# One row for the value groups and the state's update: a reordering of a fused attention and network kernel

## The chip, the cores and the metric

The kernel runs on one core of a Trainium2 chip. The metric is the device time of one launch in microseconds (us). The kernel before took 996.28 us, the median of three runs (994.85 to 998.28).

## The reference, cut to what matters

x has 4 sequences of 1024 tokens with 512 features. It is normalised (xn), and two branches are added to it.

```python
xn = layernorm(x)
q, k = rotary(xn @ Wq), rotary(xn @ Wk);  v = xn @ Wv       # 16 heads of 32
# attention with decay, by chunks of 128 tokens, for each head:
inter  = (q * q_decay) @ kv                    # kv: the state, 32 x 32
scores = (q @ k.T) * dmask                     # 128 x 128
attn   = inter + scores @ v
kv     = r_C * kv + (k * k_decay).T @ v
x1 = rms_norm(attn, rms_w) @ Wo
# a network with sparse hidden values:
z = xn @ ternary(W_syn).T + b_syn              # 2048 wide
hidden = where(z >= 204th largest of the row, relu(z), 0)
x2 = layernorm(xn + hidden @ ternary(W_out).T + b_out, gamma, beta)
out = x + x1 + x2
```

## The kernel before, in words

The 4096 tokens are 32 tiles of 128, and a tile is one chunk of the attention. After a prologue that loads and converts the weights, `run_steps` writes out 31 steps, and `last_steps` does what is left. Each engine has its own queue, whose order is written out by hand in its `step`. Semaphores are the only ties between them: `wait(eng, name, tile, per, n)` waits until the semaphore stands at tile.n x per + n. A step works on five tiles at once: a (two ahead: it is loaded and normalised), b (one ahead: q, k, v and z), t (attention, and the search for the threshold), u (one behind: threshold, hidden values, output projection) and d (two behind: the network's second product and the result).

**TensorE** (`step`, L1014): second product of the network for d, high half, the failure flag of u, low half; transposes of q; three chunks of q, k, v for b (12 products each); the state's part of the attention (`earlier_values`); scores of three groups of four heads; the output projection of u (`attention_projected`, 12 products); the first chunk of z (`projection(b, 3)`, 8 products); the scores of the fourth group; values of groups 0 and 1; second z chunk; values of groups 2 and 3; third z chunk; the update of the state (L1051); fourth z chunk; the sum of squares. The projections, z, the scores and the network use 128 columns of the array. `values` (L951) and the update (L1051) use 32 columns at a time, four heads side by side, in float32.

The scores go to three banks, `SCORES = [1, 2, 0, 1]`, so that the fourth group's bank is free when VectorE has scaled the first group (`P_ready`). The chunks of q, k, v and z share two banks, `proj`: a z chunk waits until the chunk two places ahead of it has been copied out (`qkv_out` by ScalarE for chunks 3 and 4, `z_out` by VectorE for chunks 5 and 6).

**VectorE** (`step`, L1488): last z chunk of t, flag, state, mean square, threshold of u (with a branch, for rows whose search failed), `hidden` (L1413), decayed q, statistics of a, first step of the search, result of the network for d, normalised attention, second step; then `below` (L1461), which writes all values of z under a bound to `masked`; `probs` 0 and 1, which scale the scores into `Pr`; four MAX8 (`segments`); `out_shift` of d (L1455); z chunk 0; `probs` 2 and 3; MAX8; z chunk 1; the projected attention added to x; MAX8; z chunk 2; MAX8; and `selection` (L1464 to L1486), a chain of small instructions on the 128 candidates that picks the threshold with `sel` (L1479).

`Pr` has two buffers of four heads, which the groups use in turn, so group 2 waits for the values of group 0. The same memory is `unused`, to which ScalarE's three counts write results that nobody reads; so `probs` waits for the third count (`sum3`).

**ScalarE** (`step`, L548): `diagonal`, `first_count`, `hidden_high` (L533), first copy of q (`qkv_out(b, 0)`, L427), the heads of the state (`heads_state`, L457, four instructions), `second_count` (L519), `attention_high` (L410), `normalised` (L436 and L439: x normalised in float32, and its float16 half), `third_count` (L524), `qkv_out` 1 and 2 (L427), `out_normalised` (L538, needs `out_shift`), `attention_out` (L544 and L546: the attention `aT` and its squares `sq`, both from the values' bank), `qk_high` (L447).

**GpSimd** (`step`, L736): root of the mean square (L702), decayed v (L745), decayed state (L751), root for the statistics (L634), `hidden_low` (L708), `attention_low` (L712), `low_half` (L640, needs both results of `normalised`), `out_root` of d (L716, gives `rD_ready`), biases (L645, L646), rotary (L658 to L663), `squares_added` (L721, L723), `out_scaled` and `out_added` (L728, L734), `qk_low` (L668, twice).

**SP** issues the transfers: high and low halves of the hidden values transposed, x transposed (needs `low_half`), result stored, next x loaded, q and k transposed (need `qk_low`).

Of the kernel before, what the change touches and what calls it, by code (L numbers as in the profile page):

```python
# [26 lines left out]
H, DH = 16, 32  # L27
# [5 lines left out]
NT = 32  # L33
# [17 lines left out]
def build(nc, x, Wq, Wk, Wv, Wo, rms_w, W_syn, b_syn, W_out, b_out, gamma, beta,  # L51
          t_rot, t_dmask, t_qdec, t_kdec, t_rc, t_keep, t_ident, t_iota, out):
    ctx = ExitStack()
    with ctx:
        def sb(name, shape, dt):
            return ctx.enter_context(nc.sbuf_tensor(name, shape, dt))[:]
# [54 lines left out]
        pair_a = sb("pair_a", [P, 2 * E], F32)  # L111
        aT = pair_a[:, 0:E].rearrange("p (g c) -> p g c", g=HG)
        sq = pair_a[:, E:2 * E].rearrange("p (g c) -> p g c", g=HG)
        state = sb("state", [P, P], F32)
        stateD = sb("stateD", [P, HG, P], F32)
        kvs = sb("kvs", [P, P], F32)
# [50 lines left out]
        SCORES = [1, 2, 0, 1]  # L167
# [193 lines left out]
        def _(act):  # L361
# [154 lines left out]
            def second_count(t):  # L516

                wait(act, "nt_step", t, 5, 2)
                nc.scalar.activation(unused, z[:, t.par, :], ACT.Sign, bias=nt1, accum_out=s2).then_inc(S["sum2"], 1)  # L519
# [28 lines left out]
            def step(act, i, p):  # L548
                a, b, t, u, d = (stage(i, p, k) for k in (2, 1, 0, -1, -2))
                tile0 = t.n == 0  # L550
                if u:
                    diagonal(u)
                first_count(t)
                if t.n == 1:
                    heads_state(t)
                if u:
                    hidden_high(u, masked)
                if b.n >= 3:
                    qkv_out(b, 0)
                if t.n > 1:  # L560
                    heads_state(t)
                second_count(t)
                if u:
                    attention_high(u)
                if a:
                    normalised(a)
                third_count(t)
                if tile0:
                    sums("out", (1, 2, 3, 0))
                    sign("out", out_in[2], out_other[2], out_thr[1])  # L570
                    sign("out", out_in[2], out_t[2], out_thr[0])
                else:
                    if b.n != 2:
                        qkv_out(b, 1)
                    qkv_out(b, 2)
                if d:
                    out_normalised(d)
                attention_out(t)
                if tile0:
                    act.wait_ge(S["out_tern3"], 1)  # L580
                    sign("out", out_in[1], out_other[1], out_thr[1])
                    sign("out", out_in[1], out_t[1], out_thr[0])
                qk_high(b)
                if tile0:
                    qkv_out(Tile(1, 0), 0)
                    qkv_out(Tile(1, 0), 1)

                    act.wait_ge(S["out_tern2"], 1)
                    sign("out", out_in[0], out_other[0], out_thr[1])
                    act.wait_ge(S["outT3"], 16)  # L590
                    sign("out", out_in[0], out_t[0], out_thr[0])
# [32 lines left out]
        def _(pool):  # L624
# [84 lines left out]

            def attention_low(u):  # L710
                wait(pool, "ah_ready", u, 1, 1)
                nc.gpsimd.tensor_tensor(ahl[:, 1], aT, ahl[:, 0], ALU.subtract).then_inc(S["al_ready"], 1)  # L712

            def out_root(d):
# [78 lines left out]
        def _(pe):  # L793
# [152 lines left out]
            def values(t, g):  # L946

                wait(pe, "P_ready", t, 4, g + 1)
                for j in range(4):
                    h = 4 * g + j  # L950
                    last = nc.tensor.matmul(p_av[32 * j:32 * j + 32, g * P:(g + 1) * P],  # L951
                                            v[:, t.par, h * DH:(h + 1) * DH], Pr[:, g % 2, j, :],
                                            start=False, stop=g == HG - 1, skip_group_check=True)
                last.then_inc(S["av_done"], 1)

# [58 lines left out]
            def step(pe, i, p):  # L1014
                b, t, u, d = (stage(i, p, k) for k in (1, 0, -1, -2))
                if d:
                    network_high(d)
                if u:
                    failures(u)
                if d:  # L1020
                    network_low(d)
                if t.n > 0:
                    q_transposed(t)
                if b.n > 1:
                    for n in range(2 if b.n == 2 else 0, 3):
                        projection(b, n)
                        if n == (2 if b.n == 2 else 0):
                            factors_spread(u)

                earlier_values(t)  # L1030
                scores(t, 0)
                scores(t, 1)
                scores(t, 2)
                if u:
                    attention_projected(u)
                projection(b, 3)
                scores(t, 3)
                values(t, 0)
                values(t, 1)
                projection(b, 4)  # L1040
                values(t, 2)
                values(t, 3)
                if t.n == 0:
                    sums_spread("out")
                projection(b, 5)

                wait(pe, "vd_ready", t, 1, 1)
                wait(pe, "P_ready", t, 4, 2)
                for h in range(H):
                    g, j = h // 4, h % 4  # L1050
                    last = nc.tensor.matmul(sbank[2][32 * j:32 * j + 32, g * DH:(g + 1) * DH],  # L1051
                                            qk[:, t.par, E + h * DH:E + (h + 1) * DH],
                                            vd[:, h * DH:(h + 1) * DH], start=True, stop=True)
                last.then_inc(S["kv_done"], 1)
                projection(b, 6)
                if t.n == 0:
                    projection(Tile(1, 0), 0)
                    projection(Tile(1, 0), 1)
                squares_summed(t)
# [71 lines left out]
        def _(dve):  # L1131
# [188 lines left out]
            def probs(t, g):  # L1320

                wait(dve, "scores_done", t, 4, g + 1)

                wait(dve, "av_done", t, 4, g - 1)
                wait(dve, "sum3", t, 1, 1)
                nc.vector.scalar_tensor_tensor(Pr[:, g % 2].rearrange("p j c -> p (j c)"), sbank[SCORES[g]], ppp,  # L1326
                                               dmask[:, 4 * g:4 * g + 4, :].rearrange("p j c -> p (j c)"),
                                               ALU.mult, ALU.mult).then_inc(S["P_ready"], 1)

# [158 lines left out]
            def step(dve, i, p):  # L1488
# [37 lines left out]
                below(t)  # L1526
                if tile0:
                    dve.wait_ge(S["dmask_loaded"], 16)
                probs(t, 0)
                probs(t, 1)  # L1530
                segments(t, 0)
                if d:
                    out_shift(d)
                z_chunk(b, 0)
                probs(t, 2)
                probs(t, 3)
                segments(t, 1)
                z_chunk(b, 1)
                if u:
                    attention_added(u)  # L1540
# [147 lines left out]
```

## Time and profile before

| what | value |
|---|---|
| median of three runs | 996.28 us (994.85 to 998.28) |
| the profiled execution: time, span, granted clock | 997.11 us, 994.4 us, 0.985 |
| TensorE matmul busy (instructions) | 941.7 us, 95% (6771) |
| VectorE busy | 847.6 us, 85% (2294) |
| GpSimd busy | 759.2 us, 76% (653) |
| ScalarE busy | 584.0 us, 59% (777) |
| chain that ended last, TensorE's share | 86% |

The profile is of one execution. The span is the time between the first and the last instruction on the core. Busy shares are averages over prologue, steps and tail. L12 is line 12 of the kernel; PE is TensorE, DVE VectorE, ACT ScalarE, POOL GpSimd. Consecutive matmuls overlap, so the distance from the start of one group to the start of the next is what a group costs, and not its length.

### The profile page before, as it was taken

The page shows a single profiled execution, that of the slowest core. Times are in us where ns is not written, and L with a number is a line of the kernel's source. Part 1 is how long each engine was busy: PE and PEld are TensorE (multiplying, and loading weights), DVE is VectorE, ACT ScalarE, POOL GpSimd, SP SyncE. Part 2 cuts the span into 40 slices and gives each one's busy share as a digit, 9 for nine tenths or more (in the row PEclk, how much of TensorE's full clock was granted, in tenths as well). Part 3 has the DMA queues.
Part 4 walks back from the last instruction along what each step waited for, and adds up shares of the span by engine and source line. Part 5 has one row for each costly group of instructions (what it writes and reads, how often), then busy time and mean ns, then how long its engine had stood idle before and what let it go on. Part 6 is the DMA issues. An engine that isn't in the chain of part 4 may idle for free.

```text
span 994.4 us, 19240 instructions
## 1 busy us (share of the span) xinstructions
PE 941.7 (95%) x6771; PEld 477.0 (48%) x6771; DVE 847.6 (85%) x2294; ACT 584.0 (59%) x777; POOL 759.2 (76%) x653
## 2 busy tenths in 40 slices
PE   5756999999999999999999999999999999999976
PEld 2423455555455555554555555445555554555533
DVE  6888988888888888888888888888888888888776
ACT  6769456656555565655556656555565655556641
POOL 2853798777878897778798777778887777798653
PEclk9978999999999999999999999999999999999999
DMA  9866644654655456457445654645445455445550
GB/s 323 216 231 123 122 96 79 114 110 92 118 99 107 85 94 118 95 107 118 96 94 84 112 111 91 118 100 102 90 93 117 96 107 118 96 96 83 88 96 32
DMA packets 322370, 111.07 MB, mean 112 GB/s; under 512 B 308448, under 2 KB 308704, under 8 KB 321504
## 3 DMA queue, kind: packets, MB, share of 16 engines
q1 hardware_dynamic: 318432, 102.42, 52.1%
q10 hardware_dynamic: 3840, 7.41, 2.1%
q8 instruction: 54, 0.88, 0.4%
q14 instruction: 44, 0.36, 0.1%
HBM read 24.34 MB, written 8.39 MB: 33 GB/s over the span
## 4 chain that ended last, share of the span: by engine, by line
PE 86%; DMA 4%; DVE 3%; issue 2%; POOL 2%; ACT 2%; SPq 1%; ACTq 0%; DVEq 0%; POOLq 0%
PE proj L879 44%; PE p_ffn L987 11%; PE p_ffn L993 10%; PE p_wo L1005 8%; PE p_av L951 3%; PE sbank L942 3%; PE p_av L962 3%; DMA area<-in_L_ffn_W_syn_dram 1%; PE sbank L887 1%; PE sbank L1051 1%; DMA area<-in_L_attn_Wk_dram 1%; ACT pair_b L372 1%; DMA area<-in_L_attn_Wo_dram 1%; DMA area<-hl 0%; DMA area<-area 0%
## 5 line engine op out<-in xcount | busy, mean ns | idle before, releaser
L879 PE MATMUL proj<-wqkv,xT 128*128 128x512 f16 x1152 | 259.8, 382 | 1.8 <-DVE area L1257 1.7
L879 PE MATMUL proj<-wsynT,xT 128*128 128x512 f16 x1024 | 244.5, 382 | 0.0
L879 PEld LDWEIGHTS proj<-wqkv,xT 128*128 128x128 f16 x1152 | 111.7, 98 | 129.0 <-issue 6.0
L879 PEld LDWEIGHTS proj<-wsynT,xT 128*128 128x128 f16 x1024 | 92.8, 98 | 112.6 <-issue 14.1
L708 POOL TENSOR_TENSOR hl<-area,hl 128x2048 f16<-128x2048 f32 x31 | 126.5, 4081 | 5.0 <-ACT hl L533 4.9
L1257 DVE SCALAR_TENSOR_TENSOR area<-proj,c,gb 128x512 f32<-128x512 f32 x128 | 95.3, 745 | 33.5 <-PE proj L879 30.6
L505 ACT ACTIVATE diag<-ident,c 128x128 bf16<-128x128 f32 x32 | 12.9, 402 | 187.0 <-DVE c L1342 187.0
L987 PE MATMUL p_ffn<-woutT,area 128*128 128x512 f16 x496 | 112.0, 379 | 1.9 <-DMA area<-hl 1.9
L993 PE MATMUL p_ffn<-woutT,area 128*128 128x512 f16 x496 | 112.4, 380 | 0.0
L1361 DVE MAX8 cand<-area 128x8 f32<-128x128 f32 x512 | 110.5, 279 | 0.0
L634 POOL TENSOR_TENSOR c<-c 128x1 f32<-128x1 f32 x32 | 18.6, 583 | 114.0 <-DVE c L1247 114.0
L1461 DVE SCALAR_TENSOR_TENSOR area<-area,c 128x2048 f32<-128x2048 f32 x32 | 96.3, 3009 | 5.7 <-POOL hl L708 5.5
L640 POOL TENSOR_TENSOR xhl<-xrn,xhl 128x512 f16<-128x512 f32 x32 | 83.4, 2606 | 21.5 <-ACT xhl L439 21.5
L1326 DVE SCALAR_TENSOR_TENSOR Pr<-sbank,c,dmask 128x512 f32<-128x512 f32 x128 | 90.1, 746 | 7.6 <-ACT Pr L524 3.5
L1005 PE MATMUL p_wo<-wo,ahl 128*128 128x512 f16 x384 | 90.1, 384 | 3.2 <-ACT ahl L410 1.7
L544 ACT ACTIVATE pair_a<-p_av 128x512 f32<-128x512 f32 x32 | 19.1, 596 | 103.3 <-PE p_av L951 103.3
L668 POOL TENSOR_TENSOR area<-area 128x512 f16<-128x512 f32 x64 | 73.6, 1171 | 3.5 <-ACT area L447 3.5
L987 PEld LDWEIGHTS p_ffn<-woutT,area 128*128 128x128 f16 x496 | 48.6, 102 | 53.5 <-DMA area<-hl 2.1
L1413 DVE SCALAR_TENSOR_TENSOR area<-area,c 128x2048 f32<-128x2048 f32 x31 | 73.9, 2383 | 0.0
L447 ACT ACTIVATE area<-area 128x1024 f16<-128x1024 f32 x64 | 64.1, 1049 | 14.5 <-POOL area L663 14.5
L993 PEld LDWEIGHTS p_ffn<-woutT,area 128*128 128x128 f16 x496 | 46.1, 98 | 52.2
L514 ACT ACTIVATE Pr<-area,c 128x2048 f16<-128x2048 f32 x32 | 63.6, 1988 | 8.2 <-DVE c L1301 8.2
(229 smaller groups left out, 1779.7 us busy)
## 6 DMA issues: line engine op xcount, KB each, us to landing
xrn<-in_L_attn_x_dram SPq DMA_DIRECT2D x32, 256.0 KB, 3.0
out_dram<-pair_b SPq DMA_DIRECT2D x32, 256.0 KB, 2.1
woutT<-in_L_ffn_W_syn_dram ACTq DMA_DIRECT2D x2, 1024.0 KB, 10.8
area<-in_L_ffn_W_syn_dram ACTq DMA_DIRECT2D x2, 1024.0 KB, 11.9
woutT<-in_L_ffn_W_out_dram SPq DMA_DIRECT2D x2, 1024.0 KB, 11.7
area<-in_L_attn_Wq_dram ACTq DMA_DIRECT2D x1, 1024.0 KB, 7.0
area<-in_L_attn_Wk_dram ACTq DMA_DIRECT2D x1, 1024.0 KB, 9.4
area<-in_L_attn_Wv_dram ACTq DMA_DIRECT2D x1, 1024.0 KB, 11.5
```

Source lines behind the costliest of these rows:

```text
L640: nc.gpsimd.tensor_tensor(xhl[:, 1, :], slot(xn, a), xhl[:, 0, :], ALU.subtract).then_inc(S["xl_ready"], 1)
L668: nc.gpsimd.tensor_tensor(qks[:, m, :, 2 - m, :], qk[:, b.par, m * E:(m + 1) * E].rearrange("p (h d) -> p h d", h=H), qks[:, m, :, 0, :], ...
L708: nc.gpsimd.tensor_tensor(hl[:, 1, :], src, hl[:, 0, :], ALU.subtract).then_inc(S["lo_ready"], 1)
L879: last = nc.tensor.matmul(bank, xT[:, b.par, k, :], w, start=m == 0, stop=m == len(pairs) - 1)
L987: nc.tensor.matmul(p_ffn, hT[:, k, :], woutT[:, k, :], start=k == 0, stop=False)
L993: last = nc.tensor.matmul(p_ffn, hT[:, NB + k, :], woutT[:, k, :], start=False, stop=k == NB - 1)
L1005: last = nc.tensor.matmul(p_wo, ahl[:, l, g, :], wo[:, w, g, :], start=m == 0, stop=m == len(terms) - 1)
L1257: nc.vector.scalar_tensor_tensor(z[:, b.par, n * 512:(n + 1) * 512], proj[(b.par + 3 + n) % 2], gs, gb[:, n * 512:(n + 1) * 512], ALU.mult ...
L1326: nc.vector.scalar_tensor_tensor(Pr[:, g % 2].rearrange("p j c -> p (j c)"), sbank[SCORES[g]], ppp, dmask[:, 4 * g:4 * g + 4, :].rearrange ...
L1361: nc.vector.max(cand[:, 0, 8 * n:8 * n + 8], masked[:, n * SEG:(n + 1) * SEG]).then_inc(S["seg_done"], 1)
L1413: nc.vector.scalar_tensor_tensor(dst, z[:, u.par, :], thr, z[:, u.par, :], ALU.is_ge, ALU.mult).then_inc(S["h_ready"], 1)
L1461: nc.vector.scalar_tensor_tensor(masked, z[:, t.par, :], t2, z[:, t.par, :], ALU.is_le, ALU.mult).then_inc(S["w_out"], 1)
```

## The change

All four value groups and the update of the state follow each other on TensorE, behind the second z chunk. The first z chunk goes in front of the output projection. The scaled scores of groups 2 and 3 get buffers of their own, in the memory of `aT` and `sq`; for these two, `probs` waits for `attention_low` of u (`al_ready`) and for the sum of squares of the tile before (`ss_done`), and no group waits for values any more. `attention_low` waits until `below` has run (`w_out`). On ScalarE the second count goes in front of the state's heads, the second copy (`qkv_out(b, 1)`) in front of the third count, and `normalised` behind the third count, except in step 0. On VectorE eight MAX8 and `out_shift` go in front of `probs` 0 and 1. No arithmetic is added or taken away.

```diff
@@ -111,6 +111,7 @@
         pair_a = sb("pair_a", [P, 2 * E], F32)
         aT = pair_a[:, 0:E].rearrange("p (g c) -> p g c", g=HG)
         sq = pair_a[:, E:2 * E].rearrange("p (g c) -> p g c", g=HG)
+        weighed = [Pr[:, 0], Pr[:, 1], aT, sq]
         state = sb("state", [P, P], F32)
         stateD = sb("stateD", [P, HG, P], F32)
         kvs = sb("kvs", [P, P], F32)
@@ -557,21 +558,23 @@
                     hidden_high(u, masked)
                 if b.n >= 3:
                     qkv_out(b, 0)
+                second_count(t)
                 if t.n > 1:
                     heads_state(t)
-                second_count(t)
                 if u:
                     attention_high(u)
-                if a:
+                if tile0:
                     normalised(a)
+                if b.n >= 3:
+                    qkv_out(b, 1)
                 third_count(t)
                 if tile0:
                     sums("out", (1, 2, 3, 0))
                     sign("out", out_in[2], out_other[2], out_thr[1])
                     sign("out", out_in[2], out_t[2], out_thr[0])
                 else:
-                    if b.n != 2:
-                        qkv_out(b, 1)
+                    if a:
+                        normalised(a)
                     qkv_out(b, 2)
                 if d:
                     out_normalised(d)
@@ -709,6 +712,7 @@
 
             def attention_low(u):
                 wait(pool, "ah_ready", u, 1, 1)
+                wait(pool, "w_out", u, 1, 2 if u.n < NT - 1 else 1)
                 nc.gpsimd.tensor_tensor(ahl[:, 1], aT, ahl[:, 0], ALU.subtract).then_inc(S["al_ready"], 1)
 
             def out_root(d):
@@ -949,7 +953,7 @@
                 for j in range(4):
                     h = 4 * g + j
                     last = nc.tensor.matmul(p_av[32 * j:32 * j + 32, g * P:(g + 1) * P],
-                                            v[:, t.par, h * DH:(h + 1) * DH], Pr[:, g % 2, j, :],
+                                            v[:, t.par, h * DH:(h + 1) * DH], weighed[g][:, j, :],
                                             start=False, stop=g == HG - 1, skip_group_check=True)
                 last.then_inc(S["av_done"], 1)
 
@@ -1031,19 +1035,15 @@
                 scores(t, 0)
                 scores(t, 1)
                 scores(t, 2)
+                projection(b, 3)
                 if u:
                     attention_projected(u)
-                projection(b, 3)
                 scores(t, 3)
+                projection(b, 4)
                 values(t, 0)
                 values(t, 1)
-                projection(b, 4)
                 values(t, 2)
                 values(t, 3)
-                if t.n == 0:
-                    sums_spread("out")
-                projection(b, 5)
-
                 wait(pe, "vd_ready", t, 1, 1)
                 wait(pe, "P_ready", t, 4, 2)
                 for h in range(H):
@@ -1052,6 +1052,9 @@
                                             qk[:, t.par, E + h * DH:E + (h + 1) * DH],
                                             vd[:, h * DH:(h + 1) * DH], start=True, stop=True)
                 last.then_inc(S["kv_done"], 1)
+                if t.n == 0:
+                    sums_spread("out")
+                projection(b, 5)
                 projection(b, 6)
                 if t.n == 0:
                     projection(Tile(1, 0), 0)
@@ -1321,9 +1324,12 @@
 
                 wait(dve, "scores_done", t, 4, g + 1)
 
-                wait(dve, "av_done", t, 4, g - 1)
-                wait(dve, "sum3", t, 1, 1)
-                nc.vector.scalar_tensor_tensor(Pr[:, g % 2].rearrange("p j c -> p (j c)"), sbank[SCORES[g]], ppp,
+                if g < 2:
+                    wait(dve, "sum3", t, 1, 1)
+                else:
+                    wait(dve, "al_ready", t, 1, 0)
+                    wait(dve, "ss_done", t, 1, 0)
+                nc.vector.scalar_tensor_tensor(weighed[g].rearrange("p j c -> p (j c)"), sbank[SCORES[g]], ppp,
                                                dmask[:, 4 * g:4 * g + 4, :].rearrange("p j c -> p (j c)"),
                                                ALU.mult, ALU.mult).then_inc(S["P_ready"], 1)
 
@@ -1526,15 +1532,15 @@
                 below(t)
                 if tile0:
                     dve.wait_ge(S["dmask_loaded"], 16)
+                segments(t, 0)
+                segments(t, 1)
+                if d:
+                    out_shift(d)
                 probs(t, 0)
                 probs(t, 1)
-                segments(t, 0)
-                if d:
-                    out_shift(d)
                 z_chunk(b, 0)
                 probs(t, 2)
                 probs(t, 3)
-                segments(t, 1)
                 z_chunk(b, 1)
                 if u:
                     attention_added(u)
```

## Rows read from the trace of the kernel before

**Rows 1.** Windows: each engine's busy us (instructions), clock, DMA share, GB/s.
```profile
300.00:900.00 600.00, 600.00 (x4381) 303.69 (x4380) 520.54 (x1444) 350.29 (x482) 491.18 (x421) 1.00 0.53 102
```

**Rows 2.** Timeline of TensorE in one step: start, length, engine, line, tiles, shapes.
```profile
503.24 0.83 PE L942 MATMUL sbank<-area 96*128 96x128 f16 x12
503.91 2.75 PE L1005 MATMUL p_wo<-wo,ahl 128*128 128x512 f16 x12
506.50 1.89 PE L879 MATMUL proj<-wsynT,xT 128*128 128x512 f16 x8
508.23 0.39 PE L942 MATMUL sbank<-area 96*128 96x128 f16 x4
508.55 0.64 PE L951 MATMUL p_av<-Pr,v 128*32 128x128 f32 x16
509.12 1.90 PE L879 MATMUL proj<-wsynT,xT 128*128 128x512 f16 x8
...
511.53 1.90 PE L879 MATMUL proj<-wsynT,xT 128*128 128x512 f16 x8
513.36 0.46 PE L1051 MATMUL sbank<-pair_c,area 128*32 128x32 f32 x32
513.75 1.90 PE L879 MATMUL proj<-wsynT,xT 128*128 128x512 f16 x8
```

**Rows 3.** Timeline of ScalarE in the same step.
```profile
502.37 0.80 ACT L439 ACTIVATE xhl<-xrn,c 128x512 f16<-128x512 f32 x1
503.08 1.99 ACT L524 ACTIVATE Pr<-area,c 128x2048 f16<-128x2048 f32 x1
...
505.06 0.57 ACT L427 ACTIVATE area<-proj 128x512 f32<-128x512 f32 x1
505.54 0.58 ACT L427 ACTIVATE v<-proj 128x512 f32<-128x512 f32 x1
```

**Rows 4.** Timeline of GpSimd in the same step, and one of an earlier step.
```profile
361.70 1.16 POOL L640 TENSOR_TENSOR xhl<-xrn,xhl 128x512 f16<-128x512 f32 x1
...
501.84 1.16 POOL L712 TENSOR_TENSOR ahl<-pair_a,ahl 128x512 f16<-128x512 f32 x1
503.31 2.85 POOL L640 TENSOR_TENSOR xhl<-xrn,xhl 128x512 f16<-128x512 f32 x1 [0.31 <-ACT xhl L439]
506.13 0.54 POOL L716 TENSOR_TENSOR c<-c 128x1 f32<-128x1 f32 x1
...
516.96 2.27 POOL L668 TENSOR_TENSOR area<-area 128x512 f16<-128x512 f32 x2
```

**Rows 5.** Timeline of VectorE in the same step, and of three others.
```profile
358.37 2.35 DVE L1461 SCALAR_TENSOR_TENSOR area<-area,c 128x2048 f32<-128x2048 f32 x1
...
501.97 3.18 DVE L1461 SCALAR_TENSOR_TENSOR area<-area,c 128x2048 f32<-128x2048 f32 x1 [0.23 <-POOL hl L708]
505.29 1.41 DVE L1326 SCALAR_TENSOR_TENSOR Pr<-sbank,c,dmask 128x512 f32<-128x512 f32 x2
506.62 0.86 DVE L1361 MAX8 cand<-area 128x8 f32<-128x128 f32 x4
507.40 0.19 DVE L1455 TENSOR_SCALAR c<-c 128x1 f32<-128x1 f32 x1
508.43 0.75 DVE L1257 SCALAR_TENSOR_TENSOR area<-proj,c,gb 128x512 f32<-128x512 f32 x1 [0.84 <-PE proj L879]
...
513.47 0.75 DVE L1257 SCALAR_TENSOR_TENSOR area<-proj,c,gb 128x512 f32<-128x512 f32 x1
...
517.61 0.56 DVE L1479 SCALAR_TENSOR_TENSOR sel<-iota,c,top 128x32 f32<-128x32 f32 x1
...
530.63 3.19 DVE L1461 SCALAR_TENSOR_TENSOR area<-area,c 128x2048 f32<-128x2048 f32 x1 [0.22 <-POOL hl L708]
...
947.71 0.25 DVE L1479 SCALAR_TENSOR_TENSOR sel<-iota,c,top 128x32 f32<-128x32 f32 x1
```

**Rows 6.** Timeline of TensorE in step 0: the fourth scores.
```profile
67.28 0.61 PE L942 MATMUL sbank<-area 96*128 96x128 f16 x4 [9.61 <-DVE Pr L1326]
```

## The prediction, made before the changed kernel was timed

> **What bounds the kernel now.** I read the page's busy shares first, then the window of the steady steps [rows 1], then one step of TensorE [rows 2], and then ScalarE, GpSimd and VectorE over the same 15 us [rows 3 to 5]. Rows 1 is to be read as a bound: in 600 us TensorE is busy for 600, at a granted clock of 1.00 (its upper level, 2.4 GHz). A step is the distance of two `below` rows, 530.63 - 501.97 = 28.66 us [rows 5]. TensorE has no wait in it, so a faster other engine is worth nothing here, and only a shorter instruction stream or a shorter mode change on TensorE is. VectorE is the next to bind. In a step it stands still for TensorE before chunk 0 of z, for 0.84 us [rows 5]; that is how much its own loop may grow before it sets the pace.
>
> **TensorE's stream** [rows 2]**.** No matmul is added or removed. What changes is how often the 128-column products alternate with the 32-column ones (values, state's update). A chunk of z takes 1.73 us when scores follow it (506.50 to 508.23) and 1.83 when 32-column work follows (511.53 to 513.36). Four scores take 0.67/3 = 0.22 when products of their own width follow and 0.32 ahead of values. So each entry into the 32-column form costs 0.10; there are three now and one afterwards: 0.20. A pair of value groups takes 0.57 with its way out (508.55 to 509.12). Two ways out go (after the first pair, and after the second, which is now followed by the update in the same form). The trace shows no four groups in a row, so I bound this: nothing at the least, 0.10 each at the most if leaving costs what entering does, and I take 0.10 for each, as the nearest row is the entry. TensorE's own stream becomes 28.66 - 0.40 = 28.26 (28.26 to 28.46). The Trainium skill, "TensorEngine Tiling (Array Packing)", Key Properties, says that a change of tiling mode drains the engine. The 0.10 at each entry agrees with it; by that rule alone the whole stream would be 0.40 shorter and rival B below would be the result.
>
> **`below` and the output's low half.** `below` took 3.18 us in the step shown and 2.35 in the one at 358.37 [rows 5]. In the first, GpSimd's `attention_low` had started 0.13 earlier (501.84) and ran 1.16 [rows 4]; `below` then ends 2.15 after that one's end. The new wait on `w_out` puts `attention_low` behind `below`: 2.35 instead of 3.18, so `below` ends at 504.32 instead of 505.15. `low_half` (2.85 now against 1.16 at 361.70, [rows 4]) had been held by `below` as well; it too goes back to 1.16. The Trainium skill, "SBUF — State Buffer", Who interferes with whom, states that a VectorE instruction with two SBUF inputs and a GpSimd instruction that reads SBUF exclude each other for the whole instruction, the first one winning. These rows agree; by the rule alone the edit gains 0.83 us of VectorE a step. That gain is worth only what VectorE's loop can use, and the next paragraphs say that it can't. What is queued behind the waiting `attention_low` on GpSimd: `low_half`, `out_root`, the biases, rotary, the sums of squares, the output and `qk_low`. `attention_low` ends at about 504.4 + 1.16 = 505.6, in time for the projection's last four products, which the moved z chunk puts 1.73 us later, and for the new wait of the third scaled scores.
>
> **ScalarE's order.** Second count and state's heads swap; their sum is the same, and `below` can't start earlier for the earlier count, since it already waits on GpSimd's `hidden_low` (0.23 idle, [rows 5]). So that swap is worth nothing. `normalised(a)` now has a chunk copy (0.48, 505.06 to 505.54) and the third count (1.98, 503.08 to 505.06) in front of it [rows 3]: x's high half ends at 503.17 + 2.46 = 505.63. `low_half` starts 0.14 after it, as now (503.17 to 503.31): 505.77, after 0.2 us of idle GpSimd. It takes 1.16, so `out_root` starts at 506.90 instead of 506.13 and ends at 507.44. Everything behind it on GpSimd is 0.77 later. On SP the transposes of x and of the hidden low half follow by the same 0.77; no transfer is added, and what they feed is used only in the next step's network and projections.
>
> **VectorE's order.** After `below` come eight MAX8 (0.78 for four, 506.62 to 507.40, so 1.56): ready at 505.95. Then comes `out_shift`, which waits for `out_root`; now it stands behind the first scaled scores, afterwards in front of them. It can run at 507.54 (0.10 hand-over, an estimate from the 0.14 above), so VectorE idles 1.6 us: the 0.83 from `below` and more are given back. The first scaled scores end at 507.54 + 0.15 + 0.75 = 508.44 instead of 506.04. Fourth scores need their bank: TensorE starts them at 508.54, where its stream wanted them at 508.23 or earlier. From there: scores 0.22, z chunk 1.83, values 2 x 0.57 less 0.10 to 0.20, update 0.39, so chunk 2 of z starts at 511.9 to 512.0, and VectorE takes it 1.94 later, as now (511.53 to 513.47): 513.9. That alone is a loop of 28.66 + (513.9 - 513.47) = 29.1 us. The four separate buffers remove the waits for values; with these groups' TensorE work now all behind the scaling, nothing was lost there and nothing is won.
>
> **The collision that sets the step.** `sel` (L1479) reads two SBUF inputs. Alone it takes 0.25 (947.71); in the step shown 0.56, because GpSimd's first `qk_low` had begun at 516.96 and ran till 518.12; `sel` ended at 518.17 [rows 4, 5]. `sel` comes 4.14 after chunk 2 of z: 513.9 + 4.14 = 518.0. `qk_low` comes at 516.96 + 0.77 = 517.73. So GpSimd still has the port first, but by 0.3 and not 0.65, and `sel` ends at 517.73 + 1.16 + 0.05 = 518.94, against 518.17. The loop sel, threshold, statistics, ScalarE's counts, x's high half, `low_half`, GpSimd's chain, `qk_low`, sel then closes on itself: 28.66 + 0.77 = 29.43 us, whatever TensorE does within it. TensorE (28.26) idles about 1.2 us a step, at the fourth scores.
>
> **The sum.** The loop needs a tile to normalise and one to finish, steps 2 to 29: 28 x 0.77 = 21.6. Steps 1 and 30 keep TensorE's 0.40 each: -0.8. In step 0 the first scaled scores go behind eight MAX8 (1.56), while TensorE already waits 9.61 for them [rows 6]; ScalarE's sums cover a part: +1.0 (0 to 1.56). The tail: `attention_low` of tile 30 can't start before `below` but isn't blocked in it either: 0 (-0.5 to +0.5). Profiled execution: 997.11 + 21.6 - 0.8 + 1.0 = 1018.9. It stood 0.83 over the median of 996.28, so 1018 us.
>
> **Rivals.**
> A. `sel` gets the port before `qk_low`. The point is the margin of 0.3 us (0.1 with hand-overs of 0.05): below zero, `sel` takes 0.25, and the loop is 29.1 - 0.31 = 28.8, or 28.6 with short hand-overs. 28 x (-0.06 to +0.14), with the 0.2 of the ends: 995.6 to 1001, about 998. For it: the margin is worked out over six hand-overs. Against: all of them would have to be short.
> B. The other side, faster: TensorE stays the bound, at 28.26. 30 x -0.40 + 1.0 = -11.0, 985. It decides at the fourth scores: it needs the first scaled scores by about 507.8 in this frame, so `out_shift` by 506.9, 0.6 before GpSimd can deliver. For it: today TensorE has no wait at all, and two real savings on it. Against: the order of `low_half` before `out_root`, which the edit leaves.
> C. `below` isn't freed (3.18 stays): `attention_low` ends at 506.4, and `low_half` 0.6 later than above. 28 x 1.37 = 38, 1035. Against: rows at 358.37.
> D. The loop through the fourth scores binds, with `sel`'s wait as it is now: 29.1. 28 x 0.43 = 12 + 0.2, 1009.
>
> **Chances and range.** Forecast 0.55, A 0.12, B 0.17, C 0.05, D 0.11. The forecast's own range is 1011 to 1023: a loop of 29.2 to 29.5. 8 in 10: from 991, which takes in A and D and leaves most of B, to 1023, which leaves C. A measurement can tell 0.3% (3 us) from no change: same is 993.3 to 999.3. Slower: forecast, C, D = 0.71. Same: most of A, 0.10. Faster: B and a little of A, 0.19.
>
> **What would show it.** A step of 29.4 (two `below` rows); `below` at 2.35 in all steps; `out_shift` with some 1.6 idle ahead of it, ended by L716's `rD`; TensorE idle before the fourth scores; `sel` at 0.8 to 1.1. B is right if TensorE has no idle and the step is 28.3. A, if `sel` takes 0.25 and `qk_low` 1.4. I am wrong in the mechanism if `out_shift` doesn't wait, and in the size if its wait is right but the step is under 29.

## The result, and the profile after

The changed kernel took 1016.63 us, the median of 6 runs (1014.82 to 1021.19), beside 997.83 us for the kernel before (6 runs): a ratio of 1.0197 (1.0171 to 1.0224). The forecast was 1018 us, slower.

The window first, columns as in [rows 1]: in 600 us TensorE is busy for 585 us and no longer for 600.

```profile
300.00:900.00 600.00, 585.22 (x4258) 298.88 (x4255) 502.93 (x1407) 347.07 (x478) 439.68 (x406) 1.00 0.54 99
```

Below, "the port" is short for what the rows on `below` and `sel` show: a VectorE instruction with two inputs in SBUF and a GpSimd instruction don't run at the same time, and the later one waits for the other's end. The wait stands in the trace as a longer instruction.

VectorE in one step, the lines that answer to [rows 5]. L1467 is `below`, L1461 `out_shift`, L1332 `probs`, L1260 a z chunk, L1485 `sel`:

```profile
512.86 2.35 DVE L1467 SCALAR_TENSOR_TENSOR area<-area,c 128x2048 f32<-128x2048 f32 x1 [0.96 <-POOL hl L711]
515.24 1.65 DVE L1367 MAX8 cand<-area 128x8 f32<-128x128 f32 x8
518.38 0.21 DVE L1461 TENSOR_SCALAR c<-c 128x1 f32<-128x1 f32 x1 [1.49 <-POOL c L720]
518.51 1.40 DVE L1332 SCALAR_TENSOR_TENSOR Pr<-sbank,c,dmask 128x512 f32<-128x512 f32 x2
...
524.61 0.75 DVE L1260 SCALAR_TENSOR_TENSOR area<-proj,c,gb 128x512 f32<-128x512 f32 x1 [0.63 <-PE proj L883]
...
528.75 1.08 DVE L1485 SCALAR_TENSOR_TENSOR sel<-iota,c,top 128x32 f32<-128x32 f32 x1
...
542.18 2.35 DVE L1467 SCALAR_TENSOR_TENSOR area<-area,c 128x2048 f32<-128x2048 f32 x1 [0.97 <-POOL hl L711]
```

GpSimd in the same step, answering to [rows 4] (L716 `attention_low`, L643 `low_half`, L720 `out_root`, L671 `qk_low`):

```profile
515.35 1.16 POOL L716 TENSOR_TENSOR ahl<-pair_a,ahl 128x512 f16<-128x512 f32 x1 [2.60 <-DVE area L1467]
516.68 1.16 POOL L643 TENSOR_TENSOR xhl<-xrn,xhl 128x512 f16<-128x512 f32 x1 [0.17 <-ACT xhl L440]
517.79 0.55 POOL L720 TENSOR_TENSOR c<-c 128x1 f32<-128x1 f32 x1
...
528.63 2.27 POOL L671 TENSOR_TENSOR area<-area 128x512 f16<-128x512 f32 x2
```

TensorE in the same step, answering to [rows 2] (L1009 the projected attention, L991 and L976 the network and the failure flag):

```profile
516.28 2.75 PE L1009 MATMUL p_wo<-wo,ahl 128*128 128x512 f16 x12
519.31 0.40 PE L946 MATMUL sbank<-area 96*128 96x128 f16 x4 [0.28 <-DVE Pr L1332]
519.54 1.89 PE L883 MATMUL proj<-wsynT,xT 128*128 128x512 f16 x8
521.37 0.64 PE L955 MATMUL p_av<-Pr,v 128*32 128x128 f32 x16
521.83 0.62 PE L955 MATMUL p_av<-pair_a,v 128*32 128x128 f32 x16
522.26 0.48 PE L1051 MATMUL sbank<-pair_c,area 128*32 128x32 f32 x32
522.67 3.63 PE L883 MATMUL proj<-wsynT,xT 128*128 128x512 f16 x16
...
526.39 3.61 PE L991 MATMUL p_ffn<-woutT,area 128*128 128x512 f16 x16
530.45 0.19 PE L976 MATMUL p_wo<-ones,c 128*1 128x1 f32 x2 [0.45 <-DVE c L1492]
```

These rows show a chain of four things. `out_root` (517.79 to 518.34) stands on GpSimd behind `low_half`, and `out_shift` waits 1.49 us for it. The fourth scores wait for `probs`. Chunk 2 of z is late. Then `sel` (528.75) finds the port taken by `qk_low`, which began 0.12 earlier, and takes 1.08 us instead of 0.56. A step is 542.18 - 512.86 = 29.32 us, against 28.66 [rows 5].

Where the 21.7 us of the spans (1016.1 - 994.4) came from, by the starts of `below` in both traces: 0.8 ahead of the first `below`, nothing in step 0 (38.14 before, 38.08 now), 1.4 in step 1, 18.3 in steps 2 to 29 (28 x 0.65), 0.2 in step 30, and 1.0 in the tail.

### The profile page after: what moved, and what is told of

The parts are those of the page before. It is cut to its first block, busy times and chain, and to the rows that moved or that the text cites. A ratio compares the mean times of both kernels' runs of the same rounds, so it can differ in the third digit from the quotient of the medians.

```text
span 1016.1 us, 19271 instructions
## 1 busy us (share of the span) xinstructions
PE 940.5 (93%) x6771; PEld 480.4 (47%) x6771; DVE 839.5 (83%) x2294; ACT 583.7 (57%) x777; POOL 698.9 (69%) x653
## 4 chain that ended last, share of the span: by engine, by line
DVE 28%; ACT 22%; PE 21%; issue 15%; POOL 10%; DMA 3%; DVEq 0%; SPq 0%; ACTq 0%; POOLq 0%
PE proj L883 13%; DVE area L1419 6%; ACT Pr L520 5%; ACT Pr L525 5%; DVE top L1478 3%; POOL xhl L643 3%; DVE cand L1481 3%; DVE sel L1485 3%; PE p_av L955 3%; ACT stateD L458 3%; DVE cand L1367 3%; ACT area L428 2%; DVE Pr L1332 2%; ACT xhl L440 2%; ACT xrn L437 2%
## 5 line engine op out<-in xcount | busy, mean ns | idle before, releaser
L883 PE MATMUL proj<-wsynT,xT 128*128 128x512 f16 x1024 | 240.6, 383 | 0.0
L883 PEld LDWEIGHTS proj<-wsynT,xT 128*128 128x128 f16 x1024 | 95.6, 99 | 101.6 <-issue 3.3
L1260 DVE SCALAR_TENSOR_TENSOR area<-proj,c,gb 128x512 f32<-128x512 f32 x128 | 95.3, 745 | 24.4 <-PE proj L883 24.4
L991 PE MATMUL p_ffn<-woutT,area 128*128 128x512 f16 x496 | 113.4, 382 | 2.1 <-DMA area<-hl 2.1
L1367 DVE MAX8 cand<-area 128x8 f32<-128x128 f32 x512 | 107.9, 278 | 1.1
L1467 DVE SCALAR_TENSOR_TENSOR area<-area,c 128x2048 f32<-128x2048 f32 x32 | 75.2, 2351 | 29.2 <-POOL hl L711 29.2
L716 POOL TENSOR_TENSOR ahl<-pair_a,ahl 128x512 f16<-128x512 f32 x32 | 37.1, 1160 | 90.4 <-DVE area L1467 87.7
L1009 PE MATMUL p_wo<-wo,ahl 128*128 128x512 f16 x384 | 88.5, 379 | 3.6 <-POOL ahl L716 1.8
L671 POOL TENSOR_TENSOR area<-area 128x512 f16<-128x512 f32 x64 | 74.6, 1187 | 3.5 <-ACT area L448 3.5
L991 PEld LDWEIGHTS p_ffn<-woutT,area 128*128 128x128 f16 x496 | 48.9, 103 | 54.7 <-DMA area<-hl 2.3
L1419 DVE SCALAR_TENSOR_TENSOR area<-area,c 128x2048 f32<-128x2048 f32 x31 | 72.6, 2343 | 0.0
L515 ACT ACTIVATE Pr<-area,c 128x2048 f16<-128x2048 f32 x32 | 63.6, 1988 | 8.2 <-DVE c L1304 8.2
L520 ACT ACTIVATE Pr<-area,c 128x2048 f16<-128x2048 f32 x32 | 63.7, 1992 | 1.1 <-DVE c L1426 1.1
## 6 DMA issues: line engine op xcount, KB each, us to landing
area<-in_L_ffn_W_syn_dram ACTq DMA_DIRECT2D x2, 1024.0 KB, 11.9
woutT<-in_L_ffn_W_out_dram SPq DMA_DIRECT2D x2, 1024.0 KB, 11.9
```

What stands on the lines that cost most here:

```text
L671: nc.gpsimd.tensor_tensor(qks[:, m, :, 2 - m, :], qk[:, b.par, m * E:(m + 1) * E].rearrange("p (h d) -> p h d", h=H), qks[:, m, :, 0, :], ...
L883: last = nc.tensor.matmul(bank, xT[:, b.par, k, :], w, start=m == 0, stop=m == len(pairs) - 1)
L991: nc.tensor.matmul(p_ffn, hT[:, k, :], woutT[:, k, :], start=k == 0, stop=False)
L1009: last = nc.tensor.matmul(p_wo, ahl[:, l, g, :], wo[:, w, g, :], start=m == 0, stop=m == len(terms) - 1)
L1260: nc.vector.scalar_tensor_tensor(z[:, b.par, n * 512:(n + 1) * 512], proj[(b.par + 3 + n) % 2], gs, gb[:, n * 512:(n + 1) * 512], ALU.mult ...
L1367: nc.vector.max(cand[:, 0, 8 * n:8 * n + 8], masked[:, n * SEG:(n + 1) * SEG]).then_inc(S["seg_done"], 1)
```

## The experiments

Two theories were on the bench. G: the step is set by a loop that runs from `sel` through the threshold, ScalarE's counts, `low_half` and GpSimd's queue to `qk_low`, and back to `sel` through the port. S: the late `out_shift` and `probs` cost the time by themselves, and `sel`'s wait is incidental. All times below are medians beside the kernel before on the same chip.

**e1: `out_root` in front of `low_half`.**

```diff
-                if a:
-                    low_half(a)
                 if d:
                     out_root(d)
+                if a:
+                    low_half(a)
```

> The changed kernel with GpSimd's out_root in front of low_half. Theory G (the loop through GpSimd's chain, qk_low and sel sets the step; out_shift's wait puts sel into it): out_shift's wait falls from 1.5 us to about 0.2, the fourth scores are on time, sel comes 0.4 us earlier and ends with L738 instead of with the first qk_low, and TensorE sets the step again at 28.25 to 28.3: 1016.6 - 28 x 1.03 = 987 to 989. Theory S (the late scaled scores alone set the step, sel's wait for the port plays no part): the 0.44 us of TensorE's idle before the fourth scores goes, and the step is 28.87: 1004. Neither: no change, 1016.

Measured: 1000.75 us, ratio 1.0038 (1.002 to 1.0055). `out_shift` waits 0.17 us and no longer 1.49, but the gain was 16 us (1016.63 to 1000.75) and not theory G's 29. Two rows of `sel` and the starts of `below` around them, VectorE, e1 (L1466 `below`, L1484 `sel`):

```profile
503.49 2.35 DVE L1466 SCALAR_TENSOR_TENSOR area<-area,c 128x2048 f32<-128x2048 f32 x1 [0.96 <-POOL hl L711]
...
518.94 0.32 DVE L1484 SCALAR_TENSOR_TENSOR sel<-iota,c,top 128x32 f32<-128x32 f32 x1
...
532.07 2.35 DVE L1466 SCALAR_TENSOR_TENSOR area<-area,c 128x2048 f32<-128x2048 f32 x1 [0.96 <-POOL hl L711]
...
547.63 0.25 DVE L1484 SCALAR_TENSOR_TENSOR sel<-iota,c,top 128x32 f32<-128x32 f32 x1
...
560.13 2.35 DVE L1466 SCALAR_TENSOR_TENSOR area<-area,c 128x2048 f32<-128x2048 f32 x1 [0.95 <-POOL hl L711]
```

Steps of 28.58 and 28.06 us with `sel` at 0.32 and 0.25 are followed by one of 29.26 with `sel` at 0.84: `sel` now arrives about when `qk_low` starts, sometimes before it and sometimes 0.4 behind it. Both theories had the wrong number. Removing S's cause alone leaves the collision in a part of the steps.

**e2: `sel` free of the port.** One of its two inputs is copied to PSUM first, by one small instruction (0.1 us). Nothing is reordered.

```diff
                 nc.vector.tensor_scalar(rank, s3, -0.5, TOPK - N / 2, ALU.mult, ALU.add)...
+                nc.vector.tensor_copy(sbank[2][:, 256:256 + RANKS], iota).then_inc(S["iota_ready"], 1)
...
-                nc.vector.scalar_tensor_tensor(sel, iota, rank, top, ...
+                wait(dve, "iota_ready", t, 1, 1)
+                nc.vector.scalar_tensor_tensor(sel, sbank[2][:, 256:256 + RANKS], rank, top, ...
```

> The changed kernel, in which iota is first copied to a free part of a PSUM bank (one small VectorE instruction a step, about 0.1 us), so that sel reads one SBUF input only. Order and waits stay. Theory G: sel takes 0.25 instead of 1.08, and the step falls by 0.83 - 0.1 to about 28.6: 997 (995 to 1000), with out_shift's wait of 1.5 us still there. Theory S: sel's wait plays no part; the step stays at 29.3, and the copy costs 0 to 3 us: 1016 to 1020.

Measured: 995.79 us, ratio 0.9978 (0.9961 to 0.9994). VectorE, e2 (L1461 `out_shift`, L1487 `sel`, L1408 the threshold behind the branch, L1419 `hidden`):

```profile
507.75 0.21 DVE L1461 TENSOR_SCALAR c<-c 128x1 f32<-128x1 f32 x1 [1.83 <-POOL c L720]
518.14 0.25 DVE L1487 SCALAR_TENSOR_TENSOR sel<-sbank,c,top 128x32 f32<-128x32 f32 x1
...
520.36 0.15 DVE L1408 TENSOR_SCALAR c<-c 128x1 f32<-128x1 f32 x1 [0.34 <-DVEq L1406]
...
521.19 2.75 DVE L1419 SCALAR_TENSOR_TENSOR area<-area,c 128x2048 f32<-128x2048 f32 x1
```

`out_shift` waits even longer (1.83) and yet the whole loss is gone. This decides against S: the loss needs `sel`'s wait. One caution: the 0.81 us that this step is shorter (28.51 against 29.32) aren't all `sel`'s own. `sel` ends 16.51 after the start of `below` (501.88) and no longer 16.97, which is 0.46. The other 0.35 lie behind it, where a second meeting at the port turns over as `sel` comes earlier (shown under e8).

**e3: `out_shift` behind the first two scaled scores.**

```diff
-                if d:
-                    out_shift(d)
                 probs(t, 0)
                 probs(t, 1)
+                if d:
+                    out_shift(d)
```

> The changed kernel with out_shift behind the first two scaled scores. Theory G: the fourth scores are on time, chunk 2 of z comes 0.45 us earlier, and sel then comes before the first qk_low starts and ends with L738, 1.1 us earlier; step 28.25 to 28.3: 987 to 990. Theory S: 0.44 us a step at the most: 1004.

Measured: 1007.83 us, ratio 1.0100 (1.0070 to 1.0130). Theory G's 987 to 990 is missed by 18 us. It is e1's picture with GpSimd's queue 0.1 to 0.4 us later: `qk_low` comes 15.78 and 16.12 after the start of `below`, against 15.68 in e1. Two neighbouring `sel` take 1.25 and 0.42 us, in steps of 29.66 and 28.67.

```profile
477.49 2.35 DVE L1467 SCALAR_TENSOR_TENSOR area<-area,c 128x2048 f32<-128x2048 f32 x1 [0.95 <-POOL hl L711]
493.57 1.25 DVE L1485 SCALAR_TENSOR_TENSOR sel<-iota,c,top 128x32 f32<-128x32 f32 x1
507.15 2.35 DVE L1467 SCALAR_TENSOR_TENSOR area<-area,c 128x2048 f32<-128x2048 f32 x1 [0.96 <-POOL hl L711]
522.60 0.42 DVE L1485 SCALAR_TENSOR_TENSOR sel<-iota,c,top 128x32 f32<-128x32 f32 x1
535.82 2.35 DVE L1467 SCALAR_TENSOR_TENSOR area<-area,c 128x2048 f32<-128x2048 f32 x1 [0.96 <-POOL hl L711]
```

Theory S's 1004 is under all four runs (1006.35 to 1008.44) and only just inside the interval of the ratio. Its picture, one shorter length for all steps, isn't what the rows show.

**e4: x normalised first, as before the change.** `normalised(a)` back in front of `qkv_out(b, 1)` and `third_count(t)`.

> The changed kernel with normalised back in front of the copy and the third count, where it was before the change. As predicted, the third count's and the copy's 2.46 us in front of x's high half would be the cause of GpSimd's lateness: then undoing it gives back nearly the whole 0.64 us a step, 998 to 1000. The traces of now say otherwise: low_half started only 0.17 after attention_low's end, and attention_low itself waits for below now. By that, low_half comes only 0.2 us earlier, everything behind it too, and the step is 29.1: 1011 (1009 to 1013).

Measured: 1011.45 us, ratio 1.0119 (1.0071 to 1.0166); the steps are 29.10 us. Putting `normalised` back gives a third of the lengthening (0.22 of 0.65 us a step), as the second estimate had it.

**e5: the kernel before with the row alone.** TensorE's order of values and update, and the four buffers; nothing of the other engines' orders.

```diff
-                values(t, 0)
-                values(t, 1)
                 projection(b, 4)
+                values(t, 0)
+                values(t, 1)
                 values(t, 2)
                 values(t, 3)
-                projection(b, 5)
...                                      # update of the state
+                projection(b, 5)
                 projection(b, 6)
```

> The kernel before with only the four buffers and the values and state's update in one row; ScalarE's, VectorE's and GpSimd's order, the z chunk's place and attention_low as before. If TensorE alone bounded the kernel before, as the prediction says: step 28.26, 997.8 - 30 x 0.40 + 0 = 986. If GpSimd's loop with sel was almost as long as TensorE's (sel waits 0.3 us for the port in every step of the kernel before too, and the flag is copied only 0.09 us after VectorE would be ready): the step falls by 0.1 alone, to 28.58: 995.

Measured: 992.55 us, ratio 0.9955 (0.9926 to 0.9984). The step is 28.53, not the 28.26 that the prediction gave TensorE. GpSimd's and VectorE's rows of e5 (L669 `qk_low`, L1482 `sel`):

```profile
516.38 2.28 POOL L669 TENSOR_TENSOR area<-area 128x512 f16<-128x512 f32 x2
```
```profile
516.83 0.75 DVE L1482 SCALAR_TENSOR_TENSOR sel<-iota,c,top 128x32 f32<-128x32 f32 x1
```

TensorE's own work became shorter, and `sel` came earlier and waited longer: it ends at 517.58, and the first `qk_low` at 517.54 (1.16 long). So the kernel before had a second loop of 28.53 us beside TensorE's 28.67; e7 and e9 test this.

**e6: `attention_low` unheld.** The changed kernel without the line `wait(pool, "w_out", ...)`.

> The changed kernel without attention_low's wait on w_out (it orders nothing that the data need). Theory G: below goes back to 3.2 us in most steps and ends 0.8 later, still 0.7 before VectorE's out_shift can run; low_half starts as now, since it waits for x's high half. No change: 1016 (1014 to 1019). If below's 0.83 us count, as rival C of the prediction had it: up to 28 x 0.6 more, 1033.

Measured: 1017.68 us, ratio 1.0203 (1.0158 to 1.0249): no change. `below` is back at 3.19 us, and the steps are 29.32 as with the wait.

**e7: e5 with `sel` free of the port.**

> The kernel before with the four buffers, the one row of values and update, and iota copied to PSUM so that sel reads one SBUF input. Theory G: what held e5 at 28.53 was sel's wait for the port (0.75 us); without it TensorE's stream sets the step at 28.26: 985 to 988. If e5's remainder is something else on VectorE: no gain over e5, 992, or 1 to 3 us more for the copy.

Measured: 986.63 us, ratio 0.9883 (0.9846 to 0.9919), faster than both kernels. The window (columns as in [rows 1]) and the stretch of TensorE that answers to the one above:

```profile
300.00:900.00 600.00, 600.00 (x4439) 314.21 (x4438) 526.86 (x1480) 357.20 (x490) 497.42 (x426) 1.00 0.56 103
```
```profile
503.74 0.39 PE L943 MATMUL sbank<-area 96*128 96x128 f16 x4
503.97 1.89 PE L880 MATMUL proj<-wsynT,xT 128*128 128x512 f16 x8
505.79 0.65 PE L952 MATMUL p_av<-Pr,v 128*32 128x128 f32 x16
506.25 0.62 PE L952 MATMUL p_av<-pair_a,v 128*32 128x128 f32 x16
506.69 0.48 PE L1048 MATMUL sbank<-pair_c,area 128*32 128x32 f32 x32
507.10 3.63 PE L880 MATMUL proj<-wsynT,xT 128*128 128x512 f16 x16
```

TensorE has no wait again, and does more products in the same 600 us (4439 against 4381). From the fourth scores to the third z chunk it takes 507.10 - 503.74 = 3.36 us. `below` is still at 3.19 us in this kernel: the whole gain is the row's, once nothing else holds it.

**e8: e1 with `sel` free of the port.**

> The changed kernel with out_root in front of low_half and sel free of the port. e1 alternated between steps of 28.1 and 29.3 us, with sel at 0.3 and at 0.85. Theory G: both causes are gone, every step is TensorE's 28.25 to 28.3: 986 to 989. If the alternation has another cause than the port (the branch): it stays, 995 to 1000.

Measured: 992.86 us, ratio 0.9948 (0.9931 to 0.9966), between the two cases. `sel` takes 0.25 in every step, yet steps of 28.07 and 28.68 us still alternate. What tells them apart in the trace is a second meeting at the port, behind VectorE's branch: `next_guess` (L1413), a 128x1 instruction with two SBUF inputs, and GpSimd's decayed v (L749). Two neighbouring steps, first the shorter:

```profile
491.08 0.16 DVE L1413 SCALAR_TENSOR_TENSOR c<-c 128x1 f32<-128x1 f32 x1
...
519.42 1.04 DVE L1413 SCALAR_TENSOR_TENSOR c<-c 128x1 f32<-128x1 f32 x1
```
```profile
491.22 1.05 POOL L749 TENSOR_TENSOR pair_c<-v,kdec 128x512 f32<-128x512 f32 x1
...
519.40 1.05 POOL L749 TENSOR_TENSOR pair_c<-v,kdec 128x512 f32<-128x512 f32 x1
```

In the first, `next_guess` is 0.14 ahead and takes 0.16, and `hidden` ends 3.20 after the start of decayed v. In the second it is 0.02 behind and takes 1.04, as long as decayed v lasts, and `hidden` ends 3.69 after that start: 0.5 us later. Of steps 2 to 29, the 14 under 28.1 us are all of the first kind and the 14 of 28.56 or more all of the second. No run moves decayed v alone, so this is read from the traces and not tested. TensorE waits 0.3 us for the sums of squares in every second of its turns (482.34 to 486.23, against 510.86 to 514.47).

**e9: the kernel before with `sel` free.** e2's edit, behind a wait for the update of the same step.

> The kernel before, with iota copied to PSUM so that sel reads one SBUF input (behind a wait for the state's update of the same step, which is long done). sel takes 0.25 instead of 0.56. Theory G: in the kernel before TensorE's 28.67 is the longer of the two loops, if by little, so freeing the other gives nothing: 997 (995 to 999). If the collision had cost the kernel before its 0.3 us a step: 988.

Measured: 999.79 us, ratio 1.0025 (1.0005 to 1.0045). No gain: most steps are 28.67 us, as before. The 3 us above the kernel before aren't in the steps: in the profiled execution the last `below` starts 1.3 us earlier than before, and the tail behind it takes 42.2 us at a granted clock of 0.84, against 37.2 at 0.96.

**e10: the kernel before with `attention_low` held.**

```diff
                 wait(pool, "ah_ready", u, 1, 1)
+                wait(pool, "w_out", u, 1, 2 if u.n < NT - 1 else 1)
```

> The kernel before with attention_low's wait for below (w_out) alone. below falls from 3.19 to 2.35 us in every step. If below's length counted, or was free to fall, the time falls or stays: 985 to 997. Theory G: GpSimd's low_half now starts behind attention_low at about 3.6 after below's start and ends 0.6 later than now; e5 put this loop at 28.53 beside TensorE's 28.67; with 0.6 more it is 29.1 and sets the step, with sel's wait up to 1.1: 28 x 0.45 = 13 us more, 1010 (1005 to 1014).

Measured: 1010.59 us, ratio 1.0163 (1.0108 to 1.0218). One step, GpSimd (L713 `attention_low`, L640 `low_half`, L717 `out_root`, L668 `qk_low`) and VectorE (L1462 `below`, L1480 `sel`):

```profile
511.34 1.16 POOL L713 TENSOR_TENSOR ahl<-pair_a,ahl 128x512 f16<-128x512 f32 x1 [2.60 <-DVE area L1462]
512.45 1.15 POOL L640 TENSOR_TENSOR xhl<-xrn,xhl 128x512 f16<-128x512 f32 x1
513.57 0.55 POOL L717 TENSOR_TENSOR c<-c 128x1 f32<-128x1 f32 x1
...
524.38 2.27 POOL L668 TENSOR_TENSOR area<-area 128x512 f16<-128x512 f32 x2
```
```profile
508.84 2.35 DVE L1462 SCALAR_TENSOR_TENSOR area<-area,c 128x2048 f32<-128x2048 f32 x1 [0.22 <-POOL hl L708]
...
524.53 1.05 DVE L1480 SCALAR_TENSOR_TENSOR sel<-iota,c,top 128x32 f32<-128x32 f32 x1
...
537.92 2.35 DVE L1462 SCALAR_TENSOR_TENSOR area<-area,c 128x2048 f32<-128x2048 f32 x1 [0.22 <-POOL hl L708]
```

`below` is 0.83 shorter, the step 537.92 - 508.84 = 29.08, which is 0.42 longer. This wait alone makes the kernel before 13.7 us slower (1010.59 against 996.93), of which the steps account for 28 x 0.42 = 12.

**e11: e4's and e6's edits together.**

> The changed kernel without attention_low's wait and with normalised in front of the copy and the third count: e4's and e6's edits together. e6 alone gave nothing, e4 alone 5 us. Theory G: each of the two is enough to hold low_half, so both must go; then low_half ends as in the kernel before (4.2 after below's start), out_shift has no wait although it still stands ahead of the scaled scores, and the step is e5's 28.5: 992 (989 to 996). If the two don't work together, their sum stands: 1016.6 - 5 = 1011.

Measured: 994.14 us, ratio 0.9967 (0.9946 to 0.9989); steps of 28.53. GpSimd and VectorE in one step (L1458 `out_shift`):

```profile
500.39 1.16 POOL L713 TENSOR_TENSOR ahl<-pair_a,ahl 128x512 f16<-128x512 f32 x1
501.87 2.85 POOL L641 TENSOR_TENSOR xhl<-xrn,xhl 128x512 f16<-128x512 f32 x1 [0.32 <-ACT xhl L440]
504.68 0.55 POOL L717 TENSOR_TENSOR c<-c 128x1 f32<-128x1 f32 x1
```
```profile
500.51 3.19 DVE L1464 SCALAR_TENSOR_TENSOR area<-area,c 128x2048 f32<-128x2048 f32 x1 [0.96 <-POOL hl L709]
...
505.29 0.20 DVE L1458 TENSOR_SCALAR c<-c 128x1 f32<-128x1 f32 x1
```

With both undone `out_root` comes 4.17 after `below`'s start (504.68 - 500.51), as in [rows 4, 5] (506.13 - 501.97 = 4.16), against 4.93 in the changed kernel. `out_shift` has no wait, although it still stands ahead of the scaled scores.

## Why the prediction was right, and where it wasn't

- **TensorE's stream**: right. In [rows 2] the way from the fourth scores to the last chunk is 513.75 - 508.23 = 5.52 us, with two z chunks in it; e7 has one of them there and takes 3.36. A chunk between products of its own form takes 1.73, so the same work took 5.52 - 1.73 = 3.79 before: 0.43 more. e7's steps say the same, 28.24 against 28.67. The forecast had 0.40, with 0.10 for each of four changes of form.
- **TensorE's idle time**: right in size (1.2 a step forecast), wrong in place. By the starts of its groups it is 1.08, but only 0.44 of it is at the fourth scores (516.28 to 519.31 is 3.03, against 2.59 in [rows 2]). Another 0.52 is at the failure flag, which waits for what follows `sel` (526.39 to 530.45 is 4.06, against 515.63 to 519.17 = 3.54 before), and 0.12 around the sums of squares.
- **`below` and the port**: right in size (2.35 in all steps) and right that the gain can't be used. e6 takes it away again, and the time stays the same.
- **`out_shift`'s wait**: 1.6 forecast, 1.49 measured. The MAX8 ended 4.03 after the start of `below` (516.89); the prediction's 505.95 is 3.98, while its own terms add up to 504.32 + 1.56 = 505.88.
- **The collision**: right in mechanism. `qk_low` first, `sel` 0.12 behind it (0.3 forecast) and 1.08 long (0.8 to 1.1). e2 shows it by taking the port away. The margin was smaller since VectorE took chunk 2 of z 11.75 after the start of `below` (524.61) and not 11.9. A margin of 0.12 is near to rival A, and shifts of a few tenths turn it over in e1 and e3: that it held was in part luck.
- **The size of the step**: 29.32 against 29.43. `low_half` started 3.82 after `below`'s start (516.68 - 512.86) and the forecast had 3.80 (505.77 - 501.97), so the term for GpSimd was right (0.77 both times). The missing 0.11 is the loop's starting length: it was not 28.66 but, by e5, 28.53, and 28.53 + 0.77 = 29.30. In the rows it lies between the end of `sel` and the next `below`: 12.46 before (518.17 to 530.63), 12.35 now.
- **What bounds the kernel before**: here the reading fell short. "VectorE's own loop may grow by 0.84" took one wait on TensorE for the slack of the whole loop. e5 measured 0.14. The sign was in [rows 4, 5]: `sel` already ended with `qk_low` (518.17 and 518.12), so VectorE and GpSimd were tied to each other, and a wait elsewhere in the step says nothing about that tie. The prediction closed the loop properly only for the changed kernel.
- **The cause of GpSimd's lateness**: half of it. The prediction put it on ScalarE's order and priced the new wait at nothing. e4 and e6 show that undoing either gives a third or nothing, e10 that the wait alone costs 13.7 us, e11 that both have to go. Each of the two is enough: `low_half` ends 4.77 after the start of `below` with the wait alone (e4), 4.98 with ScalarE's order alone (e6), and 4.2 with neither (e11).
- **Rival B** was priced without the collision: it asked only for `out_root` 0.6 earlier. e1 did that and reached 1000.75, not 985. TensorE's saving is real and was reached in another way (e7, 986.63). **Rival C**'s condition, a long `below` with the wait in place, didn't arise, and its 38 us weren't tested; e6 has the long `below` without the wait, and there `low_half` waits for ScalarE (2.78 us) and starts at 3.82 all the same. **Rival D** gave the late fourth scores a loop of 29.1: in e2 `out_shift` waits still longer and most steps are 28.5. The times of A, C and D were added to the profiled 997.11 and not to the median of 996.28, so they are 0.8 too high beside the forecast's.
- **The ends**: outside steps 2 to 29 the spans differ by 3.4 us, and the forecast had 0.2 (+1.0 for step 0, -0.4 each for steps 1 and 30). Step 0 took the same time, but it varies from 36.9 to 39.6 us among the traces, so they neither bear out nor refute its +1.0. Step 1 took 28.25 instead of 26.85: with e6's edit it is 27.57, with both undone (e11) 26.83, so this comes from the same two edits as the rest. The 0.8 ahead of the first `below` is scatter: e1 and e3, which differ from the changed kernel only behind that point, reach it at 63.39 and 63.24 us, the changed kernel at 65.04. The tail goes with its granted clock: 38.2 us at 0.92, against 37.2 at 0.96 before, 36.8 at 0.97 in e10 and 42.2 at 0.84 in e9.
- **The total**: the steps gave 18.3 us and not 21.6, and the ends 3.4 and not 0.2. That the spans meet the forecast's 21.8 to 0.1 is luck. The step (29.32 against 29.43) is what speaks for the mechanism.

## What to carry to other kernels

That one engine never waits is no proof that the others have room to spare. Look for an instruction whose length is set by another engine's instruction (here `sel`, 0.56 against 0.25 alone): it ties two queues into a loop. The slack of that loop, not the longest wait, says what a saving on the engine that sets the pace can bring. An edit that shortens an instruction by holding back another engine has to be priced by everything in that engine's queue behind the held one: here 0.83 us were gained on VectorE and 0.6 lost on GpSimd, and the kernel paid the loss.

## What wasn't expected of the hardware

- VectorE's idle time at the branch after the flag's load isn't fixed: 0.36 to 1.05 us in the changed kernel, for the same instructions. It costs nothing there: 26 of the 28 steps 2 to 29 are 29.30 to 29.40 us long. In each of them `next_guess`, the next instruction with two SBUF inputs, ends within 0.02 us of GpSimd's decayed v, and takes 0.36 to 1.05 us instead of 0.16. The wait for the port takes up what the branch leaves. Why the idle time differs stays open.
- Who comes first at that second meeting decides on 0.5 us of a step. In e1, e3 and e8 the steps change between the two orders: 39 steps with `next_guess` first are 27.8 to 28.5 us long, and the 45 with decayed v first are 28.6 to 29.7. e3 and e1 add the swing of `sel`, between 0.25 and 0.85 or 1.25 us. The changed kernel, e4, e5, e6, e10 and e11 have decayed v first in all of steps 2 to 29, and keep to one length but for single steps.
